# Transposed outputs and column sums by matmul, and split weights in two buffers, in a gated delta-rule layer

## What is computed

```python
qkv = silu(causal_conv4(x @ Wqkv))          # 16 heads, 128 channels each for q, k, v
z = x @ Wz; beta = sigmoid(x @ Wb); g = softplus(x @ Wa + dt_bias) * -exp(A_log)
q = l2norm(q) * 128 ** -0.5; k = l2norm(k)   # l2norm(t) = t * rsqrt(sum(t*t) + 1e-6)
for t in tokens:                             # M: 128 x 128 per sequence and head
    M = M * exp(g_t)
    M = M + outer(k_t, (v_t - k_t @ M) * b_t)
    o_t = q_t @ M
out = o * rsqrt(mean(o * o) + 1e-6) * norm_w * silu(z)
y = out @ Wout                               # summed over the heads
```

## Time and profile before

| | us |
|---|---|
| median of 3 runs | 2894.31 (2894.02 to 2895.68) |
| the profiled execution, its own time | 2893.81 |
| its span | 2891.9 |
| PE busy | 2690.6 (93%) |
| PEld busy | 2278.7 (79%) |
| DVE busy | 2257.9 (78%) |
| ACT busy | 2143.2 (74%) |
| POOL busy | 1892.7 (65%) |
| mean granted TensorE clock | 0.975 of full |

### The profile page before, as it was taken

How to read it: one execution, slowest core, us unless ns; L and a number is a source line. 1 busy time by engine, 2 the same in 40 slices (tenths; PEclk the granted TensorE clock), 3 DMA queues, 4 the chain that set the end, 5 groups by cost and what they waited for, 6 DMA issues and landing times. The chain is left out here.

```text
span 2891.9 us, 70042 instructions
## 1 busy us (share of the span) xinstructions
PE 2690.6 (93%) x23604; PEld 2278.7 (79%) x23604; DVE 2257.9 (78%) x5006; ACT 2143.2 (74%) x7286; POOL 1892.7 (65%) x1706
## 2 busy tenths in 40 slices
PE   3399999999999999999999999999999999986998
PEld 2288888888888888888888888888888888873554
DVE  5588888888888888888888888888888888853433
ACT  2388888888888888788888887888888887861211
POOL 2267777777777777777777777777777777751000
PEclk9699999999999999999999999999999999997999
DMA  5322222222222222222222222222222222201100
GB/s 190 126 87 94 89 87 77 95 89 83 82 87 96 89 81 82 96 89 80 83 96 89 87 77 95 89 83 82 87 96 89 81 82 89 89 5 53 36 29 29
DMA packets 78567, 241.78 MB, mean 84 GB/s; under 512 B 8336, under 2 KB 21520, under 8 KB 61584
## 3 DMA queue, kind: packets, MB, share of 16 engines
q1 hardware_dynamic: 78224, 237.41, 23.3%
HBM read 223.75 MB, written 13.63 MB: 82 GB/s over the span
## 5 line engine op out<-in xcount | busy, mean ns | idle before, releaser
L744 DVE SCALAR_TENSOR_TENSOR conv<-pj,cw,conv 128x511 f32<-128x511 f32 (+2 forms) x1152 | 847.0, 744 | 54.6 <-ACT conv L619 40.5
L926 PE MATMUL pj<-xt,w_hi 128*128 128x512 f32 x2048 | 694.5, 421 | 23.1 <-DVE wo L738 23.1
L539 POOL TENSOR_TENSOR kq<-kq,cum 128x512 f32<-128x512 f32 x256 | 428.1, 1693 | 0.0
L926 PEld LDWEIGHTS pj<-xt,w_hi 128*128 128x128 f32 x2048 | 354.5, 193 | 70.2 <-DVE wo L738 23.5
L926 PE MATMUL pj<-xt,w_lo 128*128 128x512 f32 x1024 | 409.3, 400 | 0.0
L568 POOL TENSOR_TENSOR inv<-inv,x 128x512 f32<-128x512 f32 x128 | 148.1, 1157 | 379.0 <-ACT inv L678 379.0
L619 ACT ACTIVATE conv<-pj,cw 128x512 f32<-128x512 f32 x384 | 266.0, 693 | 143.6 <-PE pj L926 133.4
L818 DVE TENSOR_TENSOR y<-bk,mask 128x256 f16<-128x256 f32 x512 | 216.3, 422 | 167.8 <-PE bk L992 160.3
L575 POOL TENSOR_TENSOR attn<-attn,part 128x512 f32<-128x512 f32 x256 | 326.5, 1276 | 9.0 <-ACT part L701 9.0
L638 ACT ACTIVATE squares_out<-tr 128x128 bf16<-128x128 f32 x1024 | 273.0, 299 | 47.8 <-PE tr L933 47.8
L1072 PE MATMUL pj<-wo,yt 128*128 128x256 f32 x1024 | 282.6, 399 | 0.8 <-DVE yt L869 0.8
(11 more groups left out here) (159 smaller groups left out, 7559.3 us busy)
## 6 DMA issues: line engine op xcount, KB each, us to landing
xt<-xt_scratch SPq DMA_DIRECT2D x128, 1024.0 KB, 4.8
decay<-decay_scratch SPq DMA_DIRECT2D x128, 256.0 KB, 5.3
cum<-cumdecay_scratch SPq DMA_DIRECT2D x128, 256.0 KB, 5.5
w_raw<-in_w_heads SPq DMA_DIRECT2D x16, 512.0 KB, 3.4
xt_scratch<-xt_hi SPq DMA_DIRECT2D x8, 512.0 KB, 2.8
xt_scratch<-xt_lo SPq DMA_DIRECT2D x8, 512.0 KB, 3.8
res<-in_x SPq DMA_DIRECT2D x8, 512.0 KB, 4.8
out<-yo SPq DMA_DIRECT2D x8, 512.0 KB, 3.1
```

The source lines that it names most:

```text
L539: last = nc.gpsimd.tensor_tensor(part, part, of(cum, p)[:, :], ALU.mult)
L744: nc.vector.scalar_tensor_tensor(out=conv[:, i, j:SEQ], in0=pj[:, i % 2, 0:SEQ - j], scalar=cw[:, i, p // NSEQ, TAPS - 1 - j:TAPS - j], in ...
L926: last = nc.tensor.matmul(pj[:, i % 2, :], w[:, kt, cols], x_[:, kt, :], start=(n == 0), stop=(n == 3 * KT - 1))
```

## The change

- The matmuls of `outputs` swap their operands, so o comes out with channels on partitions. `take_out`, `turn_o` and the buffer `o` go; `gated` reads bank `op`.
- q isn't turned any more: `turn_q`, its four squares and `q_norm` go. ScalarE writes `q_sq` (squares of the 512 columns of q, scaled) and `o_sq` (squares of o) in one instruction each. TensorE sums them over the partitions in `out_sums`: for each chunk two float32 matmuls with the squares as weights and one moving column `mean` (1/128), added in one PSUM column of bank `op`. `out_means` on VectorE adds the constant.
- `w_hi` and `w_lo` have two buffers each, and `split(i, head + 1)` stands in slots 1, 3, 5 and 7.
- `rhs(0)`, `norms` and `state_scale` take the form `scalar_tensor_tensor`, the first with a tensor of zeros.
- All loops have a new order and one iteration more (133); projections of pair p stand in iteration p+1, and more of a pair's steps lie an iteration later. The load of x waits for all four projections.

Cut to its core:

```diff
-    w_hi = buf(ctx, "w_hi", [P, KT, 4 * P], F32R)
-    w_lo = buf(ctx, "w_lo", [P, KT, 4 * P], F32R)
+    w_hi = [buf(ctx, f"w_hi{i}", [P, KT, 4 * P], F32R) for i in range(2)]
+    w_lo = [buf(ctx, f"w_lo{i}", [P, KT, 4 * P], F32R) for i in range(2)]
...
-                    wait(sp, proj[Z], a)
+                    for done in proj:
+                        wait(sp, done, a)
                     load_xt(a + 1)
...
+                    hi, lo = w_hi[head % 2][:, :, cols], w_lo[head % 2][:, :, cols]
                     pool.wait_ge(w_in, DMA * (head + 1))
-                    wait(pool, proj[i], NSEQ * head)
+                    wait(pool, proj[i], NSEQ * (head - 1))
...
-                    wait(pool, turned_q, p + 1)
+                    wait(pool, q_squared, p + 1)
...
@@ GpSimd's loop @@
+                scale_b(a - 2)
+                unit_diagonal(a - 2)
+                k_norm(a - 2)
+                add(0, a - 5)
+                if slot % 2:
+                    split(slot // 2, head + 1)
+                first_transpose(a - 2)
+                low_b(a - 2)
                 scale_k_tok(a - 2)
+                scale_kq(a - 3)
+                add(1, a - 5)
+                inverse(a - 3)
                 out_norm(a - 4)
...
+            def q_squares(p):
+                if real(p):
+                    wait(act, silu[Q], p + 1)
+                    wait(act, summed, p - 2)
+                    nc.scalar.activation(of(q_sq, p)[:, :], of(kq, p)[:, 1, :], ACT.Square,
+                                         scale=P * EPS ** 0.5).then_inc(q_squared, 1)
...
             def out_squares(p):
                 if real(p):
                     wait(act, o_done, p + 1)
-                    wait(act, oms_ready, p)
-                    for c in range(CH):
-                        last = nc.scalar.activation(squares_out[:, 2, c, :], op[:, c, :], ACT.Square, accum_out=so[:, c:c + 1])
-                    last.then_inc(so_ready, 1)
+                    wait(act, yt_ready, p + 1)
+                    wait(act, summed, p)
+                    nc.scalar.activation(o_sq[:, :], flat(op), ACT.Square).then_inc(o_squared, 1)
...
@@ ScalarE's loop @@
+                take_sum(0, a - 5)
+                state_input(1, a - 4)
+                take(4, a - 3)
+                high_b(a - 2)
+                take_sum(1, a - 5)
+                convolve(Q, a - 1)
+                take(5, a - 3)
+                activate(V, a - 2)
+                convolve(K, a - 1)
+                state_input(2, a - 4)
+                take(6, a - 3)
+                take_v(a - 2)
+                take(1, a - 2)
+                q_squares(a - 2)
+                activate(Q, a - 1)
+                convolve(V, a - 1)
+                activate(K, a - 1)
+                state_input(3, a - 4)
+                take(2, a - 2)
+                correction(a - 3)
+                k_squares(a - 1)
+                out_squares(a - 4)
+                state_input(0, a - 3)
+                gates(a - 1)
                 take(3, a - 2)
+                take_k(a - 1)
...
                     if c == 0:
+                        dve.wait_ge(filled, 4)
                         wait(dve, v_tok_ready, p + 1)
                         wait(dve, kn_ready, p + 1)
-                        nc.vector.tensor_scalar(r[:, 0, :], of(v_tok, p)[:, 0, :], of(kn, p)[:, 0:1], None,
-                                                ALU.mult).then_inc(r_ready[0], 1)
+                        nc.vector.scalar_tensor_tensor(out=r[:, 0, :], in0=of(v_tok, p)[:, 0, :],
+                                                       scalar=of(kn, p)[:, 0:1], in1=zeros[:, :],
+                                                       op0=ALU.mult, op1=ALU.subtract).then_inc(r_ready[0], 1)
...
+            def out_means(p):
+                if real(p):
+                    wait(dve, summed, p + 1)
                     wait(dve, oc_ready, p)
+                    dve.wait_ge(filled, 4)
+                    nc.vector.scalar_tensor_tensor(out=oms[:, :], in0=op[:, 0, 0:CH], scalar=EPS * EPS * P,
+                                                   in1=zeros[:, 0:CH], op0=ALU.add, op1=ALU.add).then_inc(oms_ready, 1)
...
-                    nc.vector.tensor_tensor(yt[:, :], flat(tr), of(gate, p)[:, :], ALU.mult).then_inc(yt_ready, 1)
+                    nc.vector.tensor_tensor(yt[:, :], flat(op), of(gate, p)[:, :], ALU.mult).then_inc(yt_ready, 1)
...
@@ VectorE's loop @@
+                mask_level(5, a - 3)
+                state(1, a - 4)
+                mask_first(a - 2)
+                convolve(Q, 1, a - 1)
+                rhs(2, a - 4)
+                convolve(Q, 2, a - 1)
+                mask_level(6, a - 3)
+                mask_level(1, a - 2)
+                convolve(K, 1, a - 1)
+                convolve(Q, 3, a - 1)
+                convolve(K, 2, a - 1)
+                state(2, a - 4)
+                convolve(K, 3, a - 1)
+                rhs(3, a - 4)
+                residual(a - 3)
+                mask_level(2, a - 2)
+                convolve(V, 1, a - 1)
+                convolve(V, 2, a - 1)
+                gated(a - 4)
                 convolve(V, 3, a - 1)
+                norms(a - 1)
                 mask_level(3, a - 2)
                 inverse_norm(a - 1)
+                state_scale(a - 1)
+                out_means(a - 4)
+                state(0, a - 3)
                 decay_b(a - 1)
                 rhs(1, a - 3)
                 mask_level(4, a - 2)
+                decay_qk(a - 1)
                 decays(a)
+                rhs(0, a - 2)
...
+            def out_sums(p):
+                if real(p):
+                    wait(pe, q_squared, p + 1)
+                    wait(pe, o_squared, p + 1)
+                    pe.wait_ge(filled, 4)
+                    for c in range(CH):
+                        nc.tensor.matmul(op[:, 0, c:c + 1], of(q_sq, p)[:, chunk(c)], mean[:, :], start=True, stop=False)
+                        last = nc.tensor.matmul(op[:, 0, c:c + 1], o_sq[:, chunk(c)], mean[:, :], start=False, stop=True)
+                    last.then_inc(summed, 1)
...
-                        nc.tensor.matmul(op[:, c, :], of(kq, p)[:, 1, chunk(c)], m[c - 1][:, :], start=True, stop=False)
-                    mm = nc.tensor.matmul(op[:, c, :], of(qk, p)[:, c, :], u[:, c, :], start=(c == 0), stop=True)
+                        nc.tensor.matmul(op[:, c, :], m[c - 1][:, :], of(kq, p)[:, 1, chunk(c)], start=True, stop=False)
+                    mm = nc.tensor.matmul(op[:, c, :], u[:, c, :], of(qk, p)[:, c, :], start=(c == 0), stop=True)
...
@@ TensorE's loop @@
+                tx_level(4, a - 3)
+                project(Q, a - 1)
+                z_level(5, a - 3)
+                state_update(1, a - 4)
+                z_first(a - 2)
+                out_bank_free(a - 4)
+                outputs(1, a - 4)
+                tx_level(5, a - 3)
+                from_state_k(2, a - 4)
+                project(K, a - 1)
+                z_level(6, a - 3)
+                solve(2, a - 4)
+                z_level(1, a - 2)
+                turn_v(a - 2)
+                tx_level(6, a - 3)
+                outputs(0, a - 4)
+                state_update(2, a - 4)
+                outputs(2, a - 4)
+                tx_level(1, a - 2)
+                residual(a - 3)
+                project(V, a - 1)
+                from_state_k(3, a - 4)
+                z_level(2, a - 2)
+                project(Z, a - 1)
+                solve(3, a - 4)
+                tx_level(2, a - 2)
+                correction(a - 3)
+                turn_k(a - 1)
                 outputs(3, a - 4, signal=o_done)
+                grams(a - 1)
+                z_level(3, a - 2)
+                solve(0, a - 3)
+                out_sums(a - 4)
+                tx_level(3, a - 2)
                 state_update(0, a - 3)
+                out_project(0, a - 4)
                 from_state_k(1, a - 3)
                 z_level(4, a - 2)
+                out_project(1, a - 4)
                 solve(1, a - 3)
```

More of the change, by code:

```diff
@@ L30 @@
 Q, K, V, Z = range(4)
-LAST_STAGE = 4
+LAST_STAGE = 5
 def level_masks():
@@ L355, in delta_heads @@
     inv = [buf(ctx, f"inv{i}", [P, CH, P]) for i in range(2)]
-    sums = [buf(ctx, f"sums{i}", [P, 2, CH]) for i in range(2)]
-    k2 = [buf(ctx, f"k2{i}", [P, 2, CH]) for i in range(2)]
+    sums = [buf(ctx, f"sums{i}", [P, CH]) for i in range(2)]
+    k2 = [buf(ctx, f"k2{i}", [P, CH]) for i in range(2)]
     kn = [buf(ctx, f"kn{i}", [P, CH]) for i in range(4)]
     f = [buf(ctx, f"f{i}", [P, CH]) for i in range(4)]
-    q2 = [buf(ctx, f"q2{i}", [P, CH]) for i in range(4)]
     m = [buf(ctx, f"m{i}", [P, P]) for i in range(CH - 1)]
@@ L414, in delta_heads @@
     m_ready = [sem(f"m_ready{i}") for i in range(CH - 1)]
-    o_done, so_ready, oms_ready, oc_ready, o_ready = (sem(s) for s in (
-        "o_done", "so_ready", "oms_ready", "oc_ready", "o_ready"))
```

(50 more changed lines are left out.)

148 lines of the change are left out of this document (31 added, 117 removed).

## The result

| | us |
|---|---|
| median before (5 runs) | 2894.22 (2891.41 to 2895.68) |
| median after (5 runs) | 2907.59 (2906.54 to 2910.5) |
| ratio | 1.0049, 95% interval 1.0037 to 1.0061 |
| span of the profiled execution, before and after | 2891.9 and 2905.6 |
| mean granted clock, before and after | 0.975 and 0.981 |

The kernel became slower by 13 us; 2934 was forecast, 40 more than before. A second set of runs of the changed kernel gave 2909.76 (ratio 1.0054, 1.0037 to 1.0071). So the sign was right, and about 26 us of the forecast did not come.

What follows compares the result with a forecast made beforehand. TensorE was taken as the bound. Period 19.48 us, 0.83 longer, times 127 gives +105; heads -67, tail +2; against the profiled 2893.8 that makes 2934 us, range 2876 to 2976.

Steps and rivals of the forecast that it cites:

- Heads, -67: At the 15 changes of head, two weight buffers remove the stall and the low clock behind it: 67 us less.
- Rival 4: The head's change stays slow because the split lengthens GpSimd's chain before `inverse`: up to +67, 3001 us; chance 5% (in parts).
- out_sums, 1.65: TensorE's 16 float32 column-sum instructions, each paced by its own weight load, add 1.65 us a pair.
- Rival 1: One-column matmuls on TensorE are nearly free: block 0.46 us, time 2797 us, faster; chance 16%.
- Waits after, 0.30 a pair: In the new loops TensorE waits for VectorE, late behind out_means: 0.30 us a pair, 0.46 at most.
- and rhs(0) for k_norm (1.02 long): VectorE's rhs(0) is held by GpSimd's k_norm and ends at 21.9; with the scan also held, 0.38 us of wait.
- Rival 2: GpSimd and VectorE do not meet, TensorE runs bare: 67 against 67, 2896 us, no change; chance 13%.
- Bare work, 19.18: TensorE's own work a pair after the change, without waits: 18.19 - 0.87 + 1.65 + 0.21 = 19.18 us.
- The 0.46 of waits: Of TensorE's 18.65 us a pair before the change, about 0.46 us were real waits for another engine.
- Tail, +2: The last pair has a longer way to the end, through out_sums and one more hand-off: +2 us.
- ScalarE, nothing: Squares and a copy come off ScalarE, which bounds nothing, so nothing comes back but shorter waits.
- Rival 3: More waits (0.6 us gives 2972 us) or a lower clock from out_sums (once in eight pairs +27); chance 12%.

Runs made afterwards that it cites:

- sums_half: The changed kernel without the eight column-sum instructions of q, the eight of o kept: 2794.53 us, ratio 0.9652.
- sums_twice: The changed kernel with the sixteen column-sum instructions of a pair issued twice, with the same result: 3365.47 us, ratio 1.1622.
- add_beside_scan: The changed kernel with k_norm and add(0) exchanged in GpSimd's loop, so a 512-column addition stands beside the scan and rhs(0): 2979.16 us, ratio 1.0292.

## Why the prediction was right in sign and 26 us too high

- *Heads, -67*: measured -66.3 alone, and -68 by the periods of the changed kernel. The boundary is gone, and with it the low clock behind it. Rival 4 is out.
- *out_sums, 1.65*: 1.70 by the rows, 0.111 an instruction by sums_half and by the shortest periods of sums_twice. The float32 load sets the pace, not the column (a step of 0.03 where the load was early, 0.112 where it was not). Rival 1 is out for float32, and holds for bfloat16.
- *Waits after, 0.30 a pair*: this is the mis-sized term, and the step that failed is "and rhs(0) for k_norm (1.02 long)". I read k_norm's length as time in which it keeps VectorE out. The trace shows 0.32 for rhs(0) in the midst of it, VectorE in time for tx_level(5), and no wait of TensorE a pair in place of 0.30. Weight loads that waited for another engine from 300 to 2500 us, 114 pairs, all of them:

```profile
PEld g L970 <- ACT b_hi L668: 0.5, 1, 0.5
PEld st L1021 <- DVE r L844: 0.2, 1, 0.2
PEld g L991 <- DVE y L809: 0.2, 1, 0.2
```

That is 0.30 x 127 = 38 us too much. add_beside_scan, where rhs(0) is held, has the wait. The other half of the sentence held: the scan was 0.29 longer. With rhs(0) not held, my own walk has VectorE in time, and that is Rival 2's mechanism; its time of 2896 was too low by what the bare sum lacked.
- *Bare work, 19.18*: with no wait left, the whole period of 19.28 is bare work. The sum was 0.10 too low, 13 us, of which 0.05 is out_sums; 38 less 13 are 25 of the 26 us. That it was so close is luck, for two terms in it were each some 0.2 wrong, in opposite directions. The 0.46 of waits that I took off the period of before was too much. Its four transposes and the solve that waits behind them take 0.88 (first block), while four such transposes without a wait take 0.47 in the changed kernel (second block) and two instructions at 0.11 another 0.22:

```profile
1505.00 0.64 PE L933 MATMUL tr<-ident,o 128*128 128x128 f32 x4
1505.56 0.49 PE L1033 MATMUL st<-r,inv 128*128 128x128 f32 x2
1505.88 0.39 PE L1054 MATMUL op<-u,qk 128*128 128x128 f32 x2
```

```profile
1514.00 0.63 PE L926 MATMUL tr<-ident,vt 128*128 128x128 f32 x4
1514.47 0.28 PE L991 MATMUL bk<-y,x 128*128 128x64 f16 x4
```

So this wait costs 0.19, though the load sat idle for 0.16. The other load of L1033 that waits 0.16 in a pair stands behind a gram matmul of 0.216 and costs 0.03. That makes 0.22 and not 0.46, and a bare 18.43 before instead of 18.19. From there, 18.43 - 0.87 + 1.70 is 19.26, which leaves 0.02 for the new order where I had 0.21.
- The Trainium skill ("SBUF — State Buffer", SBUF: two separate sides) has whichever of two such instructions starts first keep the other out until it is through. add_beside_scan agrees: 1.30 beside 512 columns. rhs(0) beside k_norm does not: 0.32 beside a power of 4 columns that is 1.05 long when nothing holds it. The measurement decides. That only the short part in which k_norm reads counts is a likely reading and not shown, since no run varied its columns.
- *Tail, +2*: 3.7 behind the last gram and 1.0 ahead of the first, against 3 saved in the first periods: 1.7 in all, near the forecast.
- *ScalarE, nothing*: 189 us came off it, 67% busy instead of 74%, and the time follows TensorE's instructions one for one (sums_half).
- *Rival 3*, a low clock: not in this kernel's steady periods (none from 131 us to the last gram; 1.00 in the period, also in the 1.70 us of one-column matmuls), but its mechanism is real one step further, in sums_twice.

What stays open: the transposes taken out (0.87) and the new order were not tried by themselves, so their share is by the count of starts alone. And why rhs(0) passes under k_norm is known only as far as the two runs on it go.

## What to carry over

Price a matmul by its weight load as well as by its columns: a float32 call is two instructions with a full load each, so a one-column sum costs as much as a 128-column product (0.11 an instruction), and in bfloat16 a quarter of that with half as many instructions. Don't take the whole length of an instruction as time in which it keeps another engine out: here 1.05 us beside VectorE cost nothing and 1.28 us beside it cost 0.56 a pair. Idle time of the row of weight loads isn't yet time lost to TensorE; distances between matmul starts show what is. And measure the parts of a double change apart: here -66 and +81 stood behind a ratio of 1.005.

## What was not expected of the hardware

- The granted clock falls while TensorE is never idle. In sums_twice out_sums is some 3.6 us of one-column float32 matmuls in a row (at the full clock). In the first period shown it starts at 1499.42 and the clock falls at 1501.50, PE being busy 6.50 of 6.50 before it; in a later one it runs from 1544.83 to 1548.4 and the clock falls at 1549.30; in the one between there is no fall. Each fall lasts 3.4 or 6.8 us at the 1.2 GHz level and costs 1.65 us for each 3.4; the mean clock is 0.912. In the changed kernel 1.7 us of the same stand in each period, and from 131 us to the last gram at 2564.6 the clock never falls.
- A GpSimd power of 4 columns (1.05 us long) lets a VectorE instruction with two SBUF tensors pass in 0.32, but is itself made 0.87 longer by the scan.
- Beside a GpSimd addition of 512 columns the same VectorE instruction takes 1.30.
- A float32 matmul with one moving column starts its successor 0.03 us later when the load is early, and 0.112 when loads follow each other.
